# Kept rows of a recurrent block: each step at a place of its own, every second place of two visits

## What is computed

```python
xn = _layernorm(x)                       # (x - mean) / sqrt(var + eps)
s = lightning_attention(xn)              # 16 heads of 128: silu(xn w_qkv), decayed blocks,
                                         # RMS norm, sigmoid gate, w_out
g = silu(ffn(xn))                        # router over 64 experts, top 8, weighted bias rows
out = x + s * g
```

## Time and profile before

| | us |
|---|---|
| median of 3 runs (lowest, highest) | 1128.8 (1127.85, 1130.4) |
| the profiled execution | 1129.56 |
| its span, first to last instruction | 1127.7 |
| TensorE matmuls busy in the span | 1097.6 |
| VectorE busy | 845.6 |
| ScalarE busy | 609.2 |
| GpSimd busy | 122.2 |

### The profile page before, as it was taken

How to read it: one execution, slowest core, us unless ns; L and a number is a source line. 1 busy time by engine, 2 the same in 40 slices (tenths; PEclk the granted TensorE clock), 3 DMA queues, 4 the chain that set the end, 5 groups by cost and what they waited for, 6 DMA issues and landing times.

```text
span 1127.7 us, 16278 instructions
## 1 busy us (share of the span) xinstructions
PE 1097.6 (97%) x6367; PEld 955.6 (85%) x6367; DVE 845.6 (75%) x1621; ACT 609.2 (54%) x1308; POOL 122.2 (11%) x115
## 2 busy tenths in 40 slices
PE   8799899999999999999999999999999999999997
PEld 6688789889898888989898887888988889898886
DVE  7687777785777868777676888868668787766757
ACT  4465465564655546464545655646555564655542
POOL 4002200000000000103010000000000000000002
PEclk8999899999999999999999999999999999999999
DMA  4333122231212222214232341311212022121403
GB/s 135 111 99 108 62 62 78 71 98 43 70 48 66 94 66 85 93 49 141 83 108 77 107 161 59 99 47 48 75 47 75 29 82 77 38 67 47 140 1 131
DMA packets 39870, 89.65 MB, mean 80 GB/s; under 512 B 4576, under 2 KB 8944, under 8 KB 39792
## 3 DMA queue, kind: packets, MB, share of 16 engines
q1 hardware_dynamic: 39792, 88.61, 24.7%
HBM read 75.98 MB, written 16.80 MB: 82 GB/s over the span
## 4 chain that ended last, share of the span: by engine, by line
PE 77%; DVE 13%; ACT 4%; DMA 3%; issue 1%; POOL 1%; SPq 0%; DVEq 0%
PE psR L217 42%; PE psB L217 18%; PE psO L217 8%; PE psS L217 8%; DMA dtab<-dscr 1%; PE psS L648 1%; DVE wvl L395 1%; ACT zh L731 1%; DVE gl L395 1%; DMA raw<-w 1%; DVE T L726 1%; DVE ql L390 1%; DVE yacc L791 1%; DVE T L673 1%; DVE wt L459 1%
## 5 line engine op out<-in xcount | busy, mean ns | idle before, releaser
L748 POOL TENSOR_TENSOR ss<-ss,sq 128x512 f32<-128x512 f32 x58 | 78.5, 1353 | 822.4 <-ACT sq L732 822.4
L217 PE MATMUL psR<-xh,gh 128*128 128x512 f32 x384 | 128.7, 416 | 4.7 <-DVE xs L981 2.6
L217 PE MATMUL psR<-xl,gh 128*128 128x512 f32 x384 | 119.3, 392 | 0.0
L217 PE MATMUL psR<-xh,gl 128*128 128x512 f32 x384 | 118.7, 390 | 0.0
L731 ACT ACTIVATE zh<-T,nw 128x512 fp32r<-128x512 f32 x64 | 46.3, 724 | 133.4 <-DVE T L726 133.4
L217 PE MATMUL psR<-wvh,xh 128*128 128x256 f32 x512 | 88.3, 295 | 6.8 <-DVE wvl L395 4.6
L217 PE MATMUL psB<-xh,gh 128*128 128x512 f32 x288 | 92.6, 403 | 1.9 <-DVE psR L558 1.2
L395 DVE TENSOR_TENSOR gl<-raw,gh 128x256 fp32r<-128x256 f32 x144 | 86.4, 601 | 6.7 <-ACT gh L394 4.4
L675 ACT ACTIVATE ph<-T 128x512 fp32r<-128x512 f32 x64 | 40.5, 632 | 90.6 <-DVE T L673 90.6
L217 PE MATMUL psB<-xl,gh 128*128 128x512 f32 x288 | 89.3, 391 | 0.0
L217 PE MATMUL psB<-xh,gl 128*128 128x512 f32 x288 | 88.8, 390 | 0.0
(11 more groups left out here) (199 smaller groups left out, 2684.4 us busy)
## 6 DMA issues: line engine op xcount, KB each, us to landing
raw<-w SPq DMA_DIRECT2D x80, 512.0 KB, 3.6
D<-dtab SPq DMA_DIRECT2D x32, 256.0 KB, 2.7
xs<-x SPq DMA_DIRECT2D x28, 256.0 KB, 3.2
dtab<-dscr SPq DMA_DIRECT2D x16, 256.0 KB
gscr<-xs SPq DMA_DIRECT2D x16, 256.0 KB, 2.0
xs<-xnorm SPq DMA_DIRECT2D x16, 256.0 KB, 3.1
out_dram<-yacc SPq DMA_DIRECT2D x16, 256.0 KB, 2.4
xs<-gscr SPq DMA_DIRECT2D x14, 256.0 KB, 3.9
```

The lines of the kernel that those rows point to most:

```text
L217: return lambda e: e.matmul(o, l, r, start=start, stop=stop, skip_group_check=shared)
L748: a = lane.do(lambda g: g.tensor_add(ss[:, j, :], ss[:, j, :], sq[:, :]), q, ss_ev.get(j))
```

## The change

`KEPT` lists the places of the statistics of tiles 8, 12, 9, 13, 10, 14, 11, 15. They move from (0,0), (0,2), (0,3), (1,0), (6,2), (6,3), (6,4), (7,0) to (0,2), (0,4), (1,1), (1,3), (6,1), (6,2), (6,3), (6,4). Every load is now two places ahead of its statistics (before, the first one was at the same place). The normalisation stays one place behind the statistics; its store to `xnorm` becomes a step of its own (`store`), one place behind the normalisation. The differences (`mingle`) come three places behind the pair's second statistics instead of two, and their two stores (`store_mingled`) one place behind the differences. No instruction is added or removed.

| step | tile 8 | 12 | 9 | 13 | pair 0 | pair 1 |
|---|---|---|---|---|---|---|
| load, before / after | (0,0) / (0,0) | (0,0) / (0,2) | (0,1) / (0,4) | (0,3) / (1,1) | | |
| statistics | (0,0) / (0,2) | (0,2) / (0,4) | (0,3) / (1,1) | (1,0) / (1,3) | | |
| normalise | (0,1) / (0,3) | (0,3) / (1,0) | (0,4) / (1,2) | (1,1) / (1,4) | | |
| store xnorm | (0,1) / (0,4) | (0,3) / (1,1) | (0,4) / (1,3) | (1,1) / (2,0) | | |
| differences | | | | | (0,4) / (1,2) | (1,2) / (2,1) |
| their stores | | | | | (0,4) / (1,3) | (1,2) / (2,2) |

The four tiles of the second set go the same way: loads from (6,0), (6,1), (6,2), (6,3) to (5,4), (6,0), (6,1), (6,2), differences stay at (7,0) and (7,2), their stores go from there to (7,1) and (7,3).

```diff
@@ -1080,31 +1080,41 @@
         def keep(tt):
-            i, ld = held.pop(tt)
-            e = normalise(tt, i, ld)
+            i, ld = held[tt]
+            held[tt] = i, normalise(tt, i, ld)
+
+        def store(tt):
+            i, e = held.pop(tt)
             xn_ev[tt] = sp.dma(xs_port[i], xnorm[tt * P:(tt + 1) * P, :], xs[:, i, :], e)
             held[("n", tt)] = i
 
-        def keep_mixed(t):
-
-            i, j = held.pop(("n", 8 + t)), held.pop(("n", 12 + t))
+        def mingle(t):
+
+            i, j = held[("n", 8 + t)], held[("n", 12 + t)]
             xa, xb = row(i), row(j)
             lo, hi = slice(0, 256), slice(256, 512)
             e = pool.do(lambda g: g.tensor_sub(xa[:, lo], xb[:, lo], xa[:, lo]), xn_ev[8 + t], xn_ev[12 + t])
             pool.do(lambda g: g.tensor_sub(xb[:, lo], xb[:, lo], xb[:, hi]), e)
             e2 = pool.do(lambda g: g.tensor_sub(xb[:, hi], xb[:, hi], xa[:, lo]), e)
-            e4 = pool.do(lambda g: g.tensor_sub(xa[:, hi], xa[:, hi], xb[:, hi]), e2)
-            for n, slot, tt in ((2 * t, i, 8 + t), (2 * t + 1, j, 12 + t)):
-                xc_ev[n] = sp.dma(xs_port[slot], xmixed[n * P:(n + 1) * P, :], xs[:, slot, :], e4)
-                xring.give(slot, xc_ev[n])
-
-        KEPT = ((0, 0), (0, 2), (0, 3), (1, 0), (6, 2), (6, 3), (6, 4), (7, 0))
+            held[("m", t)] = pool.do(lambda g: g.tensor_sub(xa[:, hi], xa[:, hi], xb[:, hi]), e2)
+
+        def store_mingled(t):
+            e = held.pop(("m", t))
+            for n, tt in ((2 * t, 8 + t), (2 * t + 1, 12 + t)):
+                i = held.pop(("n", tt))
+                xc_ev[n] = sp.dma(xs_port[i], xmixed[n * P:(n + 1) * P, :], xs[:, i, :], e)
+                xring.give(i, xc_ev[n])
+
+        KEPT = ((0, 2), (0, 4), (1, 1), (1, 3), (6, 1), (6, 2), (6, 3), (6, 4))
         for at, tt in zip(KEPT, (8, 12, 9, 13, 10, 14, 11, 15)):
-            later(*step(at, -2 if at[0] or at[1] > 1 else 0), lambda tt=tt: load(tt))
+            later(*step(at, -2), lambda tt=tt: load(tt))
             later(*at, lambda tt=tt: stat(tt, *held[tt]))
             later(*step(at), lambda tt=tt: keep(tt))
+            later(*step(at, 2), lambda tt=tt: store(tt))
         for t in range(4):
-            later(*step(KEPT[2 * t + 1], 2), lambda t=t: keep_mixed(t))
+            at = step(KEPT[2 * t + 1], 3)
+            later(*at, lambda t=t: mingle(t))
+            later(*step(at, 1), lambda t=t: store_mingled(t))
```

## The result

| | before | after |
|---|---|---|
| median (lowest, highest), us | 1128.83 (1127.85, 1130.4) | 1121.58 (1121.21, 1122.02) |
| the profiled execution | 1129.56 | 1121.52 |
| its span | 1127.7 | 1119.7 |
| mean granted clock | 0.993 | 0.997 |

The ratio is 0.9935, with a 95% interval of 0.9917 to 0.9952: faster by 7.25 us by the medians, and by 8.0 us in the two profiled executions. Forecast were 10.0 us and 1118.8. The time lies inside the range (1116.5 to 1124.5), but only because the range reached towards the rivals: the ends that the forecast worked out from its own terms, 1117.6 and 1120.0, don't hold it.

What follows compares the result with a forecast made beforehand. TensorE bounds it (busy 1097.6 of 1127.7 us); stalls of 2.45 + 0.81 + 0.6 + 4.4 and clock 2.6 make 10.9, less 0.9 added cost: 10.0 us, from median 1128.8 to 1118.8. Range 1116.5 to 1124.5.

Steps and rivals of the forecast that it cites:

- the rivals: Value weights stay late 1125.8 (0.15); GpSimd's subtractions hold VectorE 1123.0 (0.06); statistics wait for rows 1131 (0.04); no effect (0.04).
- its own terms: All costs nothing and waits gained whole, 11.2 gained, 1117.6; costs 2.0 and 0.3 of the `wvl` wait left, 8.8, 1120.0.
- stall one: TensorE's 2.45 us wait after (0,0), where VectorE's statistics wait for tile 8's rows; all 2.45 priced as gained.

Runs made afterwards that it cites:

- e3: The kernel after, with the table pair at (0,4) also waiting for `rstd` of tile 12: 1124.3 us.
- e5: The kernel after, with `KEPT` and the loads' places as before, so only the split of stores and differences is new: 1122.56 us.
- e2: The kernel before, with the table pair for visit 2 issued ahead of everything else at (0,4): 1123.79 us.
- e4: The kernel before, with the new `KEPT` places but without the split of stores and differences: 1121.51 us.
- e7: The kernel after, with statistics of tiles 9 and 13 at (2,0) and (2,2), and differences at (7,0) held for tile 15's normalisation: 1119.61 us.

## What to carry to other kernels

Ask of a load that comes late what is queued ahead of it and what that waits for: here one pair of copies behind three held stores set when a weight load two issues later could land, and moving that pair alone was worth three quarters of the gain. What follows a stall on the critical engine, here a stretch at half speed, can be slack for the others; so when the stall is removed, cost the steps near it as if their engine had no slack, by the full sum of what is put in front of the copies that free a buffer. But look first whether the other engine waits for the same load: then the stall itself gave it none. And list what leaves an engine's queue, not only what comes: on an engine that is idle most of the time, a step whose predecessor moves away runs earlier than its place, and can collide there.

## What the runs showed of the hardware

- The value weights on SP's queue were used 15.7 (e3), 16.8 (after), 17.4 (e5) and 18.1 us (e2, with three row stores in between) after the issue of the table pair ahead of them, and 8.2, 7.2, 8.1 and 7.4 after their own; 3.7 in visit 9 with no pair near. The first issue behind the pair took 4.38 us after and 5.33 in e3; the issues directly ahead of it take 0.33 to 0.43.
- Waits of 2.57 us (e2) and 2.09 us (e3) were each followed by some 3 us at the lower clock, waits of 2.45 us (before) and 1.89 us (e5) by none.
- At three places more was lost than the idle time listed in front of TensorE's matmuls: 1.46 for 0.97 at the end of visit 1, 0.62 for 0.28 at (7,0), and 2.72 for 2.45 at stall one.
- Beside four subtractions of 256 columns on GpSimd, VectorE's `pl` took 1.22 us for its usual 0.68 in three kernels (after at (7,0), e4 at (2,0), e7 at (3,0)), and TensorE lost 0.62 to 0.68 us each time. A `pl` of the same 1.22 us at 514.67 (after) cost it nothing: from unit 28 to 29 the two kernels take the same time.
